# Twelve of sixteen probability tiles a pair turned by VectorE blocks and transfers instead of TensorE, with a new order of a pair

## The reference

```python
Q = (x @ Wq.T).reshape(b, n, H, R)          # H = 8, R = 64
K = (x @ Wk.T).reshape(b, n, H, R)
V = (x @ Wv.T).reshape(b, n, H, d)          # d = 128
attn = jax.nn.softmax(jnp.einsum('bnhr,bmhr->bhnm', Q, K), axis=-1)
x = layernorm(x + jnp.einsum('bhnm,bmhd->bnd', attn, V))
h = silu(tlin(x, w1)) * tlin(x, w2)         # 128 -> 512
h = gelu(tlin(h, h1)); h = gelu(tlin(h, h2))    # 512 -> 512, twice
x = layernorm(x + tlin(h, w3))              # 512 -> 128
```

## Time and profile before

| | us |
|---|---|
| median of 3 runs | 957.55 (957.54 to 958.38) |
| the profiled execution, its device time | 958.04 |
| its span, first to last instruction | 956.2 |
| granted TensorE clock, mean | 0.996 of full speed |

### The profile page before, as it was taken

The page is one execution under the profiler, slowest core; times in us unless marked ns, Lnnn a source line. Parts: engine busy times, 40 slices in busy tenths (PEclk is TensorE's granted clock), DMA queues, the critical chain, the costliest instruction groups (busy, mean ns, idle before and its releaser), DMA issues.

```text
span 956.2 us, 19691 instructions
## 1 busy us (share of the span) xinstructions
PE 941.0 (98%) x6519; PEld 811.2 (85%) x6519; DVE 732.6 (77%) x1674; ACT 846.2 (88%) x2081; POOL 588.9 (62%) x587
## 2 busy tenths in 40 slices
PE   8999999999999999999999999999999999999996
PEld 6878888888888888888888888888888888888886
DVE  7999486886868778686796868868687786867767
ACT  7978998989989898898989989899898988999963
POOL 7955465656556575575755656565565755756753
PEclk9999999999999999999999999999999999999998
DMA  6000010100101001010100101001010010100010
GB/s 201 12 14 11 12 35 1 35 23 23 35 1 44 13 24 34 11 47 2 31 26 23 35 1 35 23 24 34 1 43 14 23 34 10 37 2 23 23 34 25
DMA packets 32998, 25.75 MB, mean 27 GB/s; under 512 B 2304, under 2 KB 27520, under 8 KB 32896
## 3 DMA queue, kind: packets, MB, share of 16 engines
q1 hardware_dynamic: 32896, 24.46, 8.4%
HBM read 16.33 MB, written 8.13 MB: 26 GB/s over the span
## 4 chain that ended last, share of the span: by engine, by line
PE 94%; DVE 2%; DMA 1%; issue 1%; ACT 1%; POOL 0%; SPq 0%; POOLq 0%; DVEq 0%; ACTq 0%
PE bank L1488 14%; PE bank L1612 13%; PE bank L1611 13%; PE bank L1482 12%; PE bank L1484 12%; PE bank L1483 12%; PE bank L1542 11%; PE bank L1591 3%; PE bank L1592 3%; DMA h_in<-in_h_t 1%; PE bank L1665 1%; PE bank L1666 1%; DVE y L1037 0%; DMA xt_in<-in_x_t 0%; DVE odd_lo L280 0%
## 5 line engine op out<-in xcount | busy, mean ns | idle before, releaser
L359 POOL TENSOR_TENSOR prob<-prob,inv_total 128x512 f32<-128x512 f32 x256 | 263.9, 1042 | 79.1 <-DVE inv_total L1006 78.8
L578 ACT ACTIVATE prob<-bank,neg_max 128x256 f32<-128x256 f32 x512 | 240.8, 491 | 10.6 <-DVE neg_max L1000 10.2
L1000 DVE TENSOR_REDUCE neg_max<-bank 128x2 f32<-128x512 f32 x256 | 170.0, 679 | 88.7 <-PE bank L1542 87.0
L280 DVE TENSOR_TENSOR pt_lo<-bank,pt_hi 128x512 fp32r<-128x512 f32 x256 | 173.5, 683 | 28.2 <-ACT pt_hi L283 25.1
L283 ACT ACTIVATE pt_hi<-bank 128x512 fp32r<-128x512 f32 x256 | 154.2, 610 | 37.4 <-PE bank L1488 30.6
L280 POOL TENSOR_TENSOR even_lo<-gelus,even_hi 128x512 fp32r<-128x512 f32 (+1 forms) x63 | 79.7, 1266 | 128.6 <-ACT even_hi L283 120.9
L1488 PE MATMUL bank<-ident,prob 128*128 128x128 f32 x1024 | 153.7, 275 | 1.8 <-POOL prob L359 0.9
L1482 PE MATMUL bank<-pt_hi,v_hi 128*128 128x256 f32 x512 | 153.7, 300 | 0.0
L1484 PE MATMUL bank<-pt_hi,v_lo 128*128 128x256 f32 x512 | 144.6, 282 | 0.0
L1483 PE MATMUL bank<-pt_lo,v_hi 128*128 128x256 f32 x512 | 144.4, 282 | 0.0
L1488 PEld LDWEIGHTS bank<-ident,prob 128*128 128x128 f32 x1024 | 120.4, 140 | 26.1 <-issue 1.5
(11 more groups left out here) (150 smaller groups left out, 2381.5 us busy)
## 6 DMA issues: line engine op xcount, KB each, us to landing
xt_in<-in_x_t SPq DMA_DIRECT2D x16, 256.0 KB, 2.6
res<-in_x SPq DMA_DIRECT2D x16, 256.0 KB, 2.9
passing<-y SPq DMA_DIRECT2D x15, 256.0 KB, 2.0
yt<-passing SPq DMA_DIRECT2D x60, 64.0 KB, 2.0
out_x<-y SPq DMA_DIRECT2D x15, 256.0 KB, 2.4
h_in<-in_h_t SPq DMA_DIRECT2D x2, 1024.0 KB, 9.6
w_in<-in_w_t SPq DMA_DIRECT2D x3, 256.0 KB, 5.2
wv_in<-in_wv_t SPq DMA_DIRECT2D x1, 512.0 KB, 4.7
```

Of the source, the lines that this page charges most:

```text
L280: return eng.tensor_tensor(dst, src, hi.bitcast(F32), ALU.subtract)
L359: nc.gpsimd.tensor_tensor(prob[:, s, :, :], prob[:, s, :, :], inv_total[:, u, :].unsqueeze(2).to_broadcast([P, NT, N]), ALU.mult).then_inc ...
L578: last = nc.scalar.activation(prob[:, slot(i, u, RING), nt, :], sc_bank(i, u)[:, nt * N:(nt + 1) * N], ACT.Exp, bias=neg_max[:, u, nt:nt + 1],
L1000: nc.vector.tensor_reduce(neg_max[:, u, :], sc_bank(i, u).rearrange("p (t m) -> p t m", m=N), AX.X, ALU.max, negate=True).then_inc(s_max, 1)
```

## The change

Of the 16 tiles of a pair, tiles 4 to 15 of pairs 1 to 14 are no longer turned on PE. They take the way that `yt` takes already: `exp` writes the exponentials in an order of 32-element runs, `norm` multiplies with the inverse sums laid out for that order, `turn_prob_blocks` turns 32x32 blocks in place in `prob` on VectorE, SyncE sends the tile to one of four buffers in device memory (`crossing`) and reads it back in four transfers straight into the slot of `pt_lo`. `pt_high` then copies from `pt_lo` to `pt_hi`, and `pt_low` subtracts in place, `pt_lo` minus `pt_hi`: both read SBUF, not PSUM. `times_v` reads both in runs of 32 elements. Tiles 0 to 3, and all tiles of pairs 0 and 15, are turned on PE as before. The order of a turn is new on all engines, and so are the bank tables.

```diff
+SENT = (4, 5, 6, 7, 8, 9, 10, 11, 12, 13, 14, 15)
-TURN_BANK = (3, 2, 3, 4, 3, 2, 5, 6, 5, 5, 4, 4, 3, 1, 5, 4)
+TURN_BANK = (4, 2, 6, 1, 0, 0, 0, 0, 0, 0, 0, 0, 0, 0, 0, 0)
...
+        LANES = 4
+        crossing = [nc.dram_tensor(f"crossing{n}", [P, TOK], F32, kind="Internal").ap() for n in range(LANES)]
...
+            def prob_out(i, u):
+                if there(i):
+                    n, times = lane(i, u)
+                    sp.wait_ge(s_blocks, sent_before(i, u + 1))
+                    need(sp, s_back[n], 16 * QUADS * (times - 1))
+                    sp.dma_start(crossing[n][:, :], whole(prob, slot(i, u, RING))).then_inc(s_out[n], 16)
+
+            def prob_back(i, u):
+                if there(i):
+                    n, times = lane(i, u)
+                    sp.wait_ge(s_out[n], 16 * times)
+                    need(sp, s_pv, after(i, J, u - 3))
+                    into = whole(pt_lo, slot(i, u, 4)).bitcast(F32)
+                    for c in range(QUADS):
+                        sp.dma_start(into[c * 32:(c + 1) * 32, :].rearrange("r (a e) -> r a e", e=P),
+                                     crossing[n][:, c * P:(c + 1) * P].rearrange("(a r) e -> r a e", r=32)).then_inc(s_back[n], 16)
...
+                    if sent(i, u):
+                        tile = whole(prob, s).rearrange("p (x t r) -> p x t r", t=NT, r=32)
+                        by = inv_total[:, u, :].unsqueeze(1).unsqueeze(3).to_broadcast([P, N // 32, NT, 32])
...
-                    need(act, s_pt_mm, after(i, J, u - RING + 1))
+                    left(act, i, u - RING)
...
+                        if sent(i, u):
+                            into = whole(prob, s).rearrange("p (c m t r) -> p t m c r", c=QUADS, m=NT, t=NT)[:, nt]
+                            scored = scored.rearrange("p (m c r) -> p m c r", m=NT, c=QUADS)
...
+                        act.wait_ge(s_back[n], 16 * QUADS * times)
+                        copy(whole(pt_hi, s), whole(pt_lo, s).bitcast(F32)).then_inc(s_pt_hi, 1)
...
+                        minus(nc.vector, whole(pt_lo, s), whole(pt_lo, s).bitcast(F32), whole(pt_hi, s)).then_inc(s_pt_lo, 1)
...
+            def turn_prob_blocks(i, u):
+                if there(i):
+                    dve.wait_ge(s_norm, after(i, J, u + 1))
+                    tile = whole(prob, slot(i, u, RING))
+                    nc.vector.transpose(tile, tile).then_inc(s_blocks, 1)
...
+                        if sent(i, u):
+                            p_hi, p_lo = (whole(p, s).rearrange("p (a m t r) -> p m t a r", a=QUADS, m=NT, t=NT)[:, mt]
+                                          for p in (pt_hi, pt_lo))
...
                     times_v(k, 2)
-                    turn_prob(k, 4, (s_exp, k, J, 7))
                     times_v(k, 3)
-                    layer4(k - 2, 0, w, (s_exp, k, J, 8))
-                layer1_z1(k - 1, 0, w, (s_x1t_lo, k - 1, 1, 1))
```

More of the change, by code:

```diff
@@ L90, in there, with sent, sent_before, turned_to @@
         return 0 <= i < PAIRS
+    def sent(i, u):
+        return u in SENT and 0 < i < LAST
+    def sent_before(i, u):
+        whole = min(max(i - 1, 0), LAST - 1) * len(SENT)
+        return whole + (sum(n < u for n in SENT) if 0 < i < LAST else 0)
+    def turned_to(i, u):
+        return i * J + u + 1 - sent_before(i, u + 1)
     def after(i, per, n):
@@ L187, in layer_kernel @@
         s_veh, s_row, s_yscaled = sem("var_eps2_last"), sem("scale_row_in"), sem("y_scaled")
+        s_blocks = sem("prob_blocks_turned")
+        s_out, s_back = ([sem(f"prob_{d}{n}") for n in range(LANES)] for d in ("out", "back"))
         block = ctx.enter_context(nc.Block())
@@ L272, in slot, with lane, left, whole @@
             return (i * J + u) % ring
+        def lane(i, u):
+            n = sent_before(i, u)
+            return n % LANES, n // LANES + 1
+        def left(eng, i, u):
+            if i * J + u >= 0:
+                i, u = divmod(i * J + u, J)
+                if sent(i, u):
+                    n, times = lane(i, u)
+                    eng.wait_ge(s_out[n], 16 * times)
+                else:
+                    eng.wait_ge(s_pt_mm, turned_to(i, u))
+        def whole(tile, s):
+            return tile[:, s, :, :].rearrange("p a b -> p (a b)")
         def hold(eng, s, value):
@@ L825, in _ @@
                 t_high(k + 1, 6)
                 gelu2(k - 1, 2)
+                pt_high(k, 15)
             high(13, 2, 2)
@@ L1335, in _ @@
                 pt_low(k, 13)
+                inverse(k + 1, 1)
                 pt_low(k, 14)
@@ new lines, in cycle @@
+                if k == 1:
+                    layer1_z1(k - 1, 1, w, (s_exp, k, J, 7))
+                else:
+                    layer1_z1(k - 1, 1, w, (s_exp, k, J, 9))
+                scores(k, 6, (s_exp, k, J, 11))
+                if k == 1:
+                    layer1_z2(k - 1, 0, w, (s_exp, k, J, 9))
+                else:
+                    layer1_z2(k - 1, 0, w, (s_x1t_lo, k - 1, 1, 1))
+                times_v(k, 4)
+                query_or_key(k + 1, 0, (s_exp, k, J, 12))
+                if k > 1:
+                    layer4(k - 2, 0, w, (s_silu, k - 1, KC, 1))
```

469 lines of the change are left out of this document (255 added, 214 removed).

## The result

| | before | after |
|---|---|---|
| median (range), us | 957.96 (957.54 to 958.74) | 966.36 (964.43 to 967.97) |
| ratio | | 1.0086 (1.0066 to 1.0106) |
| profiled execution (span), us | 958.04 (956.2) | 966.55 (964.7) |
| a steady turn, us | 58.06 | 58.64 |

A forecast was written before the change was run, and what follows sets the result against it. TensorE was taken to bound the old kernel, VectorE the new: 51.9 work + 4.1 port waits + 1.0 own waits = 57.0 us a turn, 1.06 less; 957.55 - 14 x 1.06 gives 943 us, range 908 to 985.

The forecast's parts named there:

- 51.9 + 4.1 + 1.0 = 57.0: VectorE's turn in us: work including block turns, waits at the port, and its own waits; 1.06 less than before.
- DVE's own waits: VectorE's idle time waiting for exponentials, tile 4's high part and GpSimd's roots: 1.0 us a turn, between 0 and 2.4.
- four signs that the prediction named for being wrong: `pt_lo` mean 0.7 us, block turns above 0.70 beside GpSimd, ScalarE waiting for `prob_out` landings, SyncE issuing late.
- What the prediction looked for: TensorE turns 1024 to 352, idle 4 us a turn, waits naming `pt_lo`; VectorE busiest, above 95%; `pt_lo` near 1.0 us.
- The port: Twelve two-SBUF-input low parts a turn and GpSimd hold each other off: 0.34 us a tile, 4.1 a turn.
- The stated sign: Mean of VectorE's `pt_lo` subtraction near 1.0 us (0.68 + 0.34); forecast wrong if it is 0.7.
- Rival 2: Slower: VectorE's port waits of 5.4 and own waits of 2.4 make a 59.7 us turn, 981 us; chance 0.29.
- tails behind idle time: VectorE's old 44.35 us holds some 0.08 us for each operation behind which it idled; most fall away.
- The 52.8 us of queue: TensorE's work a turn after losing twelve turned tiles, 5.3 us off the old 58.06.
- rival 1: The port costs little; TensorE and ScalarE set a turn of 54.4 us, 906 us in all; chance 0.17.
- A queue with little in it: SyncE's queue, given 25 us a turn of added issues for twelve sends and read-backs.
- the path of tile 4: Tile 4's read-back and copies against TensorE's work: one way just fits, the other makes TensorE wait 0.6 to 1.6 us.

The follow-up runs named there:

- e3: Changed kernel with one 256 KB read-back a tile instead of four of 64 KB, block placement left out: 948.9 us, ratio 0.9908.
- e5: Changed kernel with one read-back a tile and one-input low parts for sent tiles, block placement and subtraction left out: 919.1 us, ratio 0.9606.
- e1: Changed kernel with sent tiles' low parts written by a one-input VectorE instruction, subtraction left out: 953.4 us, ratio 0.996.
- e16: Changed kernel with VectorE's y normalising moved later, between block turns and row maxima, one statistics step behind `v_lo`, nothing left out: 944.8 us, ratio 0.9874.
- e21: Changed kernel with `v_low(k, 1)` ahead of the y normalising on VectorE, nothing left out: 966.9 us.
- e9: Changed kernel with SyncE's queue reordered, sends of tiles 8 and 14 ahead of earlier tiles' read-backs, nothing left out: 969.7 us.
- e4: Kernel before, with low parts of tiles 4 to 15, pairs 1 to 14, formed from two SBUF inputs, their value left out: 989.0 us, ratio 1.0328.
- e15: Changed kernel with one read-back a tile and block turns of 32 of 512 columns, placement and most turning left out: 936.7 us.
- e10: Changed kernel with four 64 KB read-backs a tile, each of 32 whole rows, block placement left out: 960.3 us, ratio 1.0027.

## Why the prediction was wrong

**Direction.** The forecast was a VectorE turn of 51.9 + 4.1 + 1.0 = 57.0 us. Measured are 54.35 us busy and 4.3 idle, 58.64. The step that failed is "DVE's own waits ... I take 1.0, between 0 and 2.4", with its reason that "an engine that runs late finds its inputs there". The chain shows where it doesn't: VectorE waits for tile 13's and tile 14's high parts and for GpSimd's root, 0.66, 1.45 and 0.38 us in the turn shown, because what it waits for came out of its own block turn: from the end of tile 14's block turn to the end of its low part are 9.2 us. The 4.3 us lie above even the 2.4 that the prediction allowed. Over the whole run VectorE waited 28.3 us for high parts of sent tiles, 2.0 a turn; its waits for exponentials make 0.9 and those for roots 0.4. Where the trip is longer than the work that VectorE has in between, running late doesn't bring its input nearer. The runs with a shorter trip show the size: 17.4 us off (e3), and 34.4 where the low parts aren't held off (e5 against e1). Of the four signs that the prediction named for being wrong, one came true: SyncE issues late. ScalarE's waits for landings of `prob_out` are 1.5 us in all; it does wait 21.6 for landings of the read-backs, which no sign named. What the prediction looked for came in part: TensorE idles 3.0 us a turn (4 forecast), VectorE is busy 93% of it (above 95), and TensorE's waits name `v_lo` (16.6 us) beside `pt_lo`.

```profile
PE bank L1603 <- DVE v_lo L317: 16.6, 13, 2.3
ACT prob L670 <- DMA crossing<-prob: 1.5, 3, 1.0
```

**The port** (VectorE and GpSimd lengthening each other). 4.1 us were forecast, all on the low parts: 12 x 0.34. Measured are 12 x 0.22 (902 less 683 ns) = 2.6, and 1.4 in a place that the sum didn't have: `y_add` 0.52 and the y normalising 4 x 0.23. The total is right by luck. The stated sign, a mean near 1.0 us, was 0.90; the forecast said it is wrong at 0.7, and that didn't happen. A normalising from SBUF to SBUF takes 645 ns where the same out of a bank takes 404, and a reduction with one input 675 ns, free of GpSimd (e1). The Trainium skill ("SBUF — State Buffer", Who interferes with whom) has rules for all three: an instruction with two SBUF inputs contends with a GpSimd instruction that reads SBUF, a scalar operation on a tensor in a two-port mode contends with GpSimd, and `tensor_reduce` never does on this chip. The three figures agree with them, though no row shows the mode of the normalising.

**What is hidden.** Rival 2 set the turning point at 6.2 us of hold-offs and idle time in a turn; 4.1 + 4.3 = 8.4 passed it, though VectorE's busy time came out 1.65 lower than the terms give (51.9 + 4.1 would be 56.0, 54.35 were busy). The prediction had a reason for that, tails behind idle time that fall away; no run tests it. Its mechanism is the nearest of those written down; its 59.7 us were too many.

**TensorE.** `bank<-ident,prob` fell to 352 as forecast. The 52.8 us of queue are not shown by themselves: e5, with the later costs mostly gone, has TensorE on the chain at 55.3 us a turn, 0.9 more than the 54.4 of rival 1, and busy 54.5 of it, in which short waits are hidden. e5 gains 39.0 us on the kernel before, so a saving was there and was spent. Reading runs of 32 elements costs no time: the products of `times_v` start 0.12 us apart as before. ScalarE's high parts out of SBUF took 651 ns for 607 out of a bank, 0.5 us a turn that was put at nothing. "Block turns 0.70", "lands in 2.0" and "1.75 for four issues" held (0.696, 2.1 and 2.2, 4 x 0.432 = 1.73).

**SyncE.** "A queue with little in it" was true on average, 25 us a turn, and wrong where it mattered: the sends and read-backs crowd into some 40 us, and I worked out the path of tile 4 alone, where it just fits. Tile 14's send has tile 13's four issues ahead of it, and its read-back tile 15's send and one of y.

**The order.** The change itself moved `norm2(k - 3)` from behind `v_low(k, 1)` and `t_low(k, 7)` to the front of `v_low(k, 1)`. I costed it at nothing. Moved out of the stretch it gives 21.5 us (e16), swapped with `v_lo` alone nothing (e21).

Shown by runs: taking away the hold-offs of the low parts, the four small read-backs or the early y work turns the sign, each alone (e1, e3, e16). Not settled: how the 8.4 us divide among them, for they overlap (13.0 + 17.4 against 47.3); whether the issues without the pieces' shape would turn it, about 11 of the 17 us; whether e16 gains by the place or by the hold-off that ends with it; and why e9 lost 3 us.

## What to carry to other kernels

When work leaves the bound engine for a round trip (block turn, send, read-back, copy, subtract), add up that trip for the last item of a batch as well as the first, with every issue ahead of it in the one queue, and set it against the work that the receiving engines have in the meantime; the mean occupancy of a queue, 25 us of 58 here, hid it. An in-order engine with 13.7 us of idle time a turn is no cover for 6 us of delays if others wait for what stands behind them (e4). Once a new engine carries the chain, look through its queue for work that nobody waits for and move it away before judging the change, since the old order was fitted to another bound.

## What the runs showed of the hardware

- VectorE's instructions with two SBUF inputs and GpSimd's lengthen each other. VectorE's of 128 x 512 went from a mean of 683 ns to 902 here and 1197 in e4, one to 1.8 us; GpSimd's multiplication from 1042 to 1125, and 1159 in e15. A one-input reduction of the same size is free of it on both sides (675 and 1041 in e1).
- A normalising of 128 x 128 from SBUF to SBUF, one tensor input, is held off as well: four in 1.07 us with GpSimd idle (e16), 2.46 beside two multiplications. From a bank all 64 took 400 to 411 ns, with GpSimd busy 65% of the span.
- An issue on SyncE's queue takes 0.32 us (median) for 256 KB in whole rows (e3), 0.42 for 64 KB in whole rows (e10) and 0.43 in 512-byte pieces. In these rows more bytes don't lengthen it.
- Two delays can hide each other: removing one gave 13 us, removing the other 17, removing both 47.
